# VectorE adds a group's turned rows to X one round later, in the last stage's end of a four-layer kernel

## The chip, the cores and the metric

The kernel runs on one core of one Trainium2 chip. The metric is the device time of one execution in microseconds (us). The time given for a kernel is the median of several runs on the chip; one further execution was profiled, and all rows of the trace come from that one.

## What is computed

Four layers work on x of shape (2, 2048, 128), each wrapped as x + layernorm(layer(layernorm(x))): a time mix, a chain of ternary products, a state space model, and a mixture of experts. Only the last one matters here:

```python
logits = x @ gate_w + gate_b                      # 8 experts
probs = softmax(logits)
top_w, top_idx = top_k(probs, 2)
top_w = top_w / sum(top_w)
h = silu(x @ w1[e]) * (x @ w3[e])
out_e = h @ w2[e]
out = sum over the two experts of top_w * out_e
x = x + layernorm(out)
```

## The kernel before, in words

X stands in SBUF for the whole kernel, features on the 128 partitions and the 4096 positions (2 x 2048) along the free axis. The last stage, phase_moe, sorts the positions by expert, multiplies tiles of 256 gathered rows on TensorE, and scatters the result rows to a table in DRAM (moe_outs), two rows for each position. What follows is the end of the stage, where the change is.

There the 4096 positions go in 8 groups (GROUPS) of 512, each as 4 chunks (TC) of 128 positions. Here a position is a partition and its 128 features lie along the free axis. For each group five engines work one after the other:

- SyncE loads the group's two rows per position from moe_outs (line 1883, 512 KB, a semaphore back0 to back7 for each group; all eight are issued at once). The tile is called room.
- VectorE, add_up (lines 2413 to 2424): the weighted sum of the two rows of each position with its total, four instructions (line 2418), and the negated mean (line 2423, minus). The sums go to `total`, four buffers in the memory of hid, so add_up of group i waits until GpSimd has scaled group i-4.
- ScalarE, spread (line 2128): squares about the mean, four instructions. VectorE, weigh (line 2428), multiplies the sum of squares by the share. ScalarE, inverse_spread (lines 2134 and 2137): Ln and Exp, the inverse root. VectorE, scale_of (line 2433): the factor of the group.
- GpSimd (line 2190), four instructions: (total + minus) * scale, into `scaled`, two buffers in the memory of sq. Group i waits for its factor and, from group 2 on, until TensorE has turned group i-2.
- TensorE (line 2036): turns the four 128x128 blocks by a product with the identity, in f32, into one half of the PSUM tile R1 (pR in the profile), the half i % 2. Group i waits for the scaled rows and, from group 2 on, until VectorE has added group i-2 (semaphore addedC). The profile counts eight matmul records for a group.
- VectorE, add_out (line 2439): X plus the turned rows, 128x512. Then SyncE stores the group's part of X (line 1887, 256 KB).

VectorE's four kinds of work are interleaved by a loop written out by hand, and this sets their order, as each engine works through its instructions in order:

```python
            for i in range(GROUPS + 3):
                if i < GROUPS:
                    add_up(i)
                if 1 <= i <= GROUPS:
                    weigh(i - 1)
                if 2 <= i <= GROUPS + 1:
                    scale_of(i - 2)
                if i >= 3:
                    add_out(i - 3)
```

One pass of this loop is called a round; round i begins with the sums of group i. ScalarE's own loop does spread(i) and then inverse_spread(i-1). GpSimd and TensorE take the groups one after the other.

Of the kernel before, what the change touches and what calls it, by code (L numbers as in the profile page):

```python
# [1741 lines left out]
def phase_moe(nc, G):  # L1742
# [5 lines left out]
    GROUPS = NT * B  # L1748
# [16 lines left out]
    with mem:  # L1765
# [100 lines left out]
        def tile_of(i):  # L1866
            return i % B, ds(i // B)
# [327 lines left out]
        def _(dve):  # L2195
# [202 lines left out]
            for n in range(UNITS):  # L2398
                i, u = divmod(n, 2)
# [12 lines left out]
            def add_up(i):  # L2412
                dve.wait_ge(S[f"back{i}"], 16)
                if i >= 4:
                    dve.wait_ge(S["scaledC"], i - 3)
                for j in range(TC):
                    c = i * TC + j
                    last = nc.vector.scalar_tensor_tensor(out=total[:, i % 4, j, :], in0=back[:, 1, c, :],
                                                          scalar=ratio[:, c:c + 1], in1=back[:, 0, c, :],
                                                          op0=ALU.mult, op1=ALU.add, accum_out=sums[:, c:c + 1])  # L2420
                last.then_inc(S["summed"], 1)
                dve.wait_ge(S["summed"], i + 1)
                nc.vector.tensor_scalar(minus[:, slab(i)], sums[:, slab(i)], -1.0 / P, None, ALU.mult)\
                  .then_inc(S["minus"], 1)

            def weigh(i):
                dve.wait_ge(S["squaredC"], i + 1)
                nc.vector.tensor_tensor(var[:, slab(i)], var[:, slab(i)], squared_share[:, slab(i)], ALU.mult)\
                  .then_inc(S["weighted"], 1)

            def scale_of(i):
                dve.wait_ge(S["rstdC"], i + 1)
                nc.vector.tensor_tensor(scale[:, slab(i)], var[:, slab(i)], share[:, slab(i)], ALU.mult)\
                  .then_inc(S["scale"], 1)

            def add_out(i):
                b, t = tile_of(i)
                dve.wait_ge(S["turnedC"], i + 1)
                nc.vector.tensor_tensor(X[:, b, t], X[:, b, t], R1[:, i % 2, :], ALU.add).then_inc(S["addedC"], 1)

            dve.wait_ge(S["squared_share"], 1)
            for i in range(GROUPS + 3):
                if i < GROUPS:
                    add_up(i)
                if 1 <= i <= GROUPS:
                    weigh(i - 1)
                if 2 <= i <= GROUPS + 1:
                    scale_of(i - 2)
                if i >= 3:
                    add_out(i - 3)  # L2450


# [57 lines left out]
```

## Time and profile before

| | us |
|---|---|
| median of 3 runs | 1417.13 |
| lowest and highest run | 1414.95 and 1420.96 |
| the profiled execution, its own time | 1412.45 |
| its span in the trace | 1410.5 |
| TensorE busy | 1131.2 (80%) |
| VectorE busy | 1012.6 (72%) |
| ScalarE busy | 784.9 (56%) |
| GpSimd busy | 726.6 (52%) |
| mean granted clock of TensorE | 0.90 |

The span runs from the first to the last instruction of the profiled execution; its own time is 1.95 us more. In the rows PE is TensorE, PEld its weight load, DVE VectorE, ACT ScalarE, POOL GpSimd, SP SyncE, and L2418 is line 2418 of the kernel. PEclk is the clock granted to TensorE as a share of its full rate. The last landed scatter stands about 1371.6 us after the start of the span, and the end of the stage runs from there to 1410.5 us. The shares of the whole span say little of it.

### The profile page before, as it was taken

The page shows a single profiled execution, that of the slowest core. Times are in us where ns is not written, and L with a number is a line of the kernel's source. Part 1 is how long each engine was busy: PE and PEld are TensorE (multiplying, and loading weights), DVE is VectorE, ACT ScalarE, POOL GpSimd, SP SyncE. Part 2 cuts the span into 40 slices and gives each one's busy share as a digit, 9 for nine tenths or more (in the row PEclk, how much of TensorE's full clock was granted, in tenths as well). Part 3 has the DMA queues.
Part 4 walks back from the last instruction along what each step waited for, and adds up shares of the span by engine and source line. Part 5 has one row for each costly group of instructions (what it writes and reads, how often), then busy time and mean ns, then how long its engine had stood idle before and what let it go on. Part 6 is the DMA issues. An engine that isn't in the chain of part 4 may idle for free. (4 is left out here: it accounts for less than half of the span.)

```text
span 1410.5 us, 16938 instructions
## 1 busy us (share of the span) xinstructions
PE 1131.2 (80%) x5010; PEld 563.6 (40%) x5010; DVE 1012.6 (72%) x1417; ACT 784.9 (56%) x1269; POOL 726.6 (52%) x611
## 2 busy tenths in 40 slices
PE   6554689999999988888898989896675587877764
PEld 2221234444444333333333333332233475756664
DVE  5996765656645379999999999999927654444444
ACT  5755545646554468686777768674434243333344
POOL 0122351323312038887978888877631466565554
PEclk8886889999999989999999999999986698898885
DMA  6000000000000001000000000000001011111214
GB/s 210 0 1 0 0 1 0 1 1 0 0 0 1 0 31 30 16 16 15 16 16 15 30 0 0 0 0 1 0 8 53 27 39 43 38 41 39 40 52 163
DMA packets 13866, 33.26 MB, mean 24 GB/s; under 512 B 3584, under 2 KB 3776, under 8 KB 13568
## 3 DMA queue, kind: packets, MB, share of 16 engines
q1 hardware_dynamic: 8368, 21.34, 4.5%
q0 software_dynamic: 4992, 10.23, 2.7%
q8 instruction: 39, 0.64, 0.2%
q10 hardware_dynamic: 432, 0.76, 0.2%
q14 instruction: 35, 0.29, 0.1%
HBM read 23.01 MB, written 9.31 MB: 23 GB/s over the span
## 5 line engine op out<-in xcount | busy, mean ns | idle before, releaser
L1632 POOL TENSOR_TENSOR prod<-hs,csb 128x1024 f32<-128x1024 f32 x128 | 301.9, 2359 | 178.0 <-DVE hs L1682 176.7
L1682 DVE TENSOR_TENSOR_SCAN hs<-dA,carry,pD 128x512 f32<-128x512 f32 x256 | 313.8, 1267 | 5.5 <-DVE pD L1697 0.8
L1440 PE MATMUL pY<-prod,const 128*128 128x512 f32 x512 | 245.2, 601 | 11.2 <-DVE h L1667 7.4
L1547 ACT ACTIVATE dA<-dt,negA 128x512 f32<-128x512 f32 x256 | 169.9, 716 | 1.4 <-DVE dt L1734 1.4
L2403 DVE SCALAR_TENSOR_TENSOR hid<-pR,silu 128x512 f32<-128x512 f32 x78 | 53.8, 690 | 131.1 <-ACT silu L2114 83.5
L1440 PEld LDWEIGHTS pY<-prod,const 128*128 128x128 f32 x512 | 96.5, 192 | 122.0 <-issue 107.5
L1558 ACT ACTIVATE csb<-pC 128x512 f32<-128x512 f32 x128 | 76.0, 594 | 108.1 <-PE pC L1453 108.0
L2180 POOL DMA_INDIRECT moe_outs<-y,to x78 | 81.7, 1048 | 85.0 <-ACT y L2106 62.1
L2114 ACT ACTIVATE silu<-pR 128x512 f32<-128x512 f32 x78 | 46.5, 596 | 121.5 <-remote 52.3
L2160 POOL DMA_INDIRECT g<-moe_rows,source x78 | 81.9, 1050 | 48.9 <-DVE source L2352 25.8
L1893 PE MATMUL pR<-x,moe_hi 128*128 128x256 f16 x312 | 93.9, 301 | 15.6 <-DVE x L2387 5.9
L979 ACT ACTIVATE stage<-pR,vec 128x512 f32<-128x512 f32 x64 | 43.9, 687 | 100.1 <-PE pR L679 100.0
L1894 PE MATMUL pR<-x,moe_hi 128*128 128x256 f16 x312 | 93.5, 300 | 3.0 <-issue 3.0
L1895 PE MATMUL pR<-x,moe_lo 128*128 128x256 f16 x312 | 93.1, 298 | 2.7 <-issue 2.4
L1697 DVE TENSOR_TENSOR pD<-dtu,pD 128x1024 f32<-128x1024 f32 x64 | 78.5, 1227 | 6.0 <-PE pD L1450 0.9
L2010 PE MATMUL pY<-moe_hi,hid_lo 128*128 x312 | 64.3, 235 | 11.4 <-issue 11.4
L2009 PE MATMUL pY<-moe_lo,hid_hi 128*128 x312 | 63.9, 234 | 9.0 <-issue 9.0
L1392 PE MATMUL pQ<-xn,convw 128*128 128x512 f32 x112 | 59.1, 653 | 14.7 <-DVE xn L1660 14.7
L1453 PE MATMUL pC<-split,sel 96*128 96x512 bf16 x128 | 50.1, 391 | 24.4 <-ACT csb L1558 24.4
L2008 PE MATMUL pY<-moe_hi,hid_hi 128*128 x312 | 63.9, 234 | 4.9 <-issue 4.1
L1450 PE MATMUL pD<-split,sel 96*128 96x512 bf16 x128 | 50.3, 393 | 21.0 <-DVE hs L1682 20.9
L421 POOL TENSOR_TENSOR o<-o,rs 128x512 f32<-128x512 f32 x8 | 12.3, 1531 | 104.0 <-DVE o L541 104.0
(401 smaller groups left out, 2719.8 us busy)
## 6 DMA issues: line engine op xcount, KB each, us to landing
raw<-moe_w SPq DMA_DIRECT2D x12, 512.0 KB, 3.6
room<-moe_outs SPq DMA_DIRECT2D x8, 512.0 KB, 7.9
hidw<-hid_w SPq DMA_DIRECT2D x1, 2048.0 KB, 10.0
moe_rows<-xt SPq DMA_DIRECT2D x8, 256.0 KB, 2.0
outT<-X SPq DMA_DIRECT2D x8, 256.0 KB, 2.0
X<-xT SPq DMA_DIRECT2D x3, 512.0 KB, 4.2
g<-moe_rows,source POOLq DMA_INDIRECT x78
moe_outs<-y,to POOLq DMA_INDIRECT x78
```

Source lines behind the costliest of these rows:

```text
L1440: last = nc.tensor.matmul(YB[c][:], G.ident, prod[:, slot(b, n), c, :], start=n == 0, stop=n == DST - 1)
L1547: last = nc.scalar.activation(dA[:, slot(b, n), c, :], dt[:, b, c, :], ACT.Exp, scale=negA[:, c, n:n + 1])
L1558: nc.scalar.activation(csb[:, slot(b, n), 0, :], CC[:], ACT.Copy).then_inc(S["c_in"], 1)
L1632: nc.gpsimd.tensor_tensor(prod[:, slot(b, n), :, :], hs[:, slot(b, n), :, :], csb[:, slot(b, n), :, :].to_broadcast([P, CB, N]), ALU.mult)\
L1682: last = nc.vector.tensor_tensor_scan(hs[:, slot(b, n), c, :], dA[:, slot(b, n), c, :], dBu(n, c), carry[:, b, n, c:c + 1], ALU.mult, ALU.add)
L1697: last = nc.vector.tensor_tensor(DD[:, 0:CB, :], dtu[:, b, :, :], bcastB(n).unsqueeze(1).to_broadcast([P, CB, N]), ALU.mult)
L1893: nc.tensor.matmul(out, w_hi, x_hi, start=start, stop=False)
L1894: nc.tensor.matmul(out, w_hi, x_lo, start=False, stop=False)
L1895: return nc.tensor.matmul(out, w_lo, x_hi, start=False, stop=stop)
L2010: last = nc.tensor.matmul(out, hid_lo[:, n % HR, at], w_hi, start=False, stop=u == 1 and h == 1 and r == 1)
L2160: nc.gpsimd.indirect_dma_start(g[:, i % GR, r, :], None, rows, bass.IndirectOffsetOnAxis(ap=source[:, 2 * i + r:2 * i + r + 1], axis=0))\
L2180: nc.gpsimd.indirect_dma_start(outs, bass.IndirectOffsetOnAxis(ap=to[:, 2 * i + r:2 * i + r + 1], axis=0), y[:, i % YR, r, :], None).then_ ...
```

## The change

Only VectorE's loop is changed. The loop has one round more, and the add of a group's turned rows stands at the end of round i+4 in place of round i+3.

```diff
-            for i in range(GROUPS + 3):
+            for i in range(GROUPS + 4):
                 if i < GROUPS:
                     add_up(i)
                 if 1 <= i <= GROUPS:
                     weigh(i - 1)
                 if 2 <= i <= GROUPS + 1:
                     scale_of(i - 2)
-                if i >= 3:
-                    add_out(i - 3)
+                if i >= 4:
+                    add_out(i - 4)
```

The instructions of the other engines and their order are the same. First place: VectorE at round 3, the first that had an add. L2418 are the sums of a group (four instructions), L2423 the mean, L2428 the weighing, L2433 the factors, L2439 the add.

```order
@@ -1060,5 +1060,4 @@
 L2428 TENSOR_TENSOR var<-var,squared_share 128x4
 L2433 TENSOR_TENSOR scale<-var,share 128x4
-L2439 TENSOR_TENSOR X<-X,pR_4 128x512
 L2418 SCALAR_TENSOR_TENSOR hid,sums<-room,ratio 128x128 x4
 L2423 TENSOR_SCALAR minus<-sums 128x4
```

The add of group 0 is gone from between the factors of group 1 and the sums of group 4. In every later round the same five kinds stand in the same places, with the add of the group before.

Second place: VectorE's last rounds, from the factors of group 7 on.

```order
@@ -1085,4 +1084,4 @@
 L2439 TENSOR_TENSOR X<-X,pR_4 128x512
 L2433 TENSOR_TENSOR scale<-var,share 128x4
-L2439 TENSOR_TENSOR X<-X,pR_4 128x512 x2
+L2439 TENSOR_TENSOR X<-X,pR_4 128x512 x3
 L1765 UNCONDITIONAL_BRANCH
```

The factors of group 7 stood behind six adds and two followed; now they stand behind five, and three follow.

## Rows read from the trace of the kernel before

**Rows 1.** The chain that ended last, from 1386 us: start us, us, what

```profile
1386.00 2.15 issue
...
1388.20 2.03 POOL sq L2190 x4
...
1390.28 2.09 PE pR L2036 x8
...
1392.40 2.14 issue
...
1401.51 4.00 PE pR L2036 x16
...
1405.53 0.69 DVE X L2439
```

**Rows 2.** TensorE in order of time, 1380 to 1411 us: [idle before, what ended it]

```profile
1383.87 3.79 PE L2036 MATMUL pR<-const,sq 128*128 128x128 f32 x16 [19.06 <-POOL sq L2190]
1390.28 4.06 PE L2036 MATMUL pR<-const,sq 128*128 128x128 f32 x16 [2.62 <-POOL sq L2190]
1396.68 4.06 PE L2036 MATMUL pR<-const,sq 128*128 128x128 f32 x16 [2.34 <-POOL sq L2190]
1401.51 3.98 PE L2036 MATMUL pR<-const,sq 128*128 128x128 f32 x16 [0.78 <-POOL sq L2190]
```

**Rows 3.** Waits, 1370 to 1411 us: who waited for whom, total, times, longest

```profile
PE pR L2036 <- POOL sq L2190: 24.8, 4, 19.1
POOL sq L2190 <- DVE scale L2433: 18.4, 7, 11.5
...
DVE X L2439 <- PE pR L2036: 10.8, 6, 2.3
```

**Rows 4.** VectorE in order of time, 1386 to 1395 us, same columns as rows 2

```profile
1386.59 0.35 DVE L2418 SCALAR_TENSOR_TENSOR hid<-room,ratio 128x128 f32<-128x128 f32 x1
...
1388.61 0.34 DVE L2418 SCALAR_TENSOR_TENSOR hid<-room,ratio 128x128 f32<-128x128 f32 x1
...
1390.22 0.15 DVE L2433 TENSOR_TENSOR scale<-var,share 128x4 f32<-128x4 f32 x1
1392.39 0.69 DVE L2439 TENSOR_TENSOR X<-X,pR 128x512 f32<-128x512 f32 x1 [2.02 <-PE pR L2036]
1392.99 0.34 DVE L2418 SCALAR_TENSOR_TENSOR hid<-room,ratio 128x128 f32<-128x128 f32 x1
```

**Rows 5.** ScalarE in order of time, 1384 to 1393 us, same columns

```profile
1385.21 0.21 ACT L2137 ACTIVATE var<-var 128x4 f32<-128x4 f32 x1
...
1390.28 0.40 ACT L2128 ACTIVATE convw<-hid,minus 128x128 f32<-128x128 f32 x1 [0.21 <-DVE minus L2423]
...
1392.15 0.20 ACT L2137 ACTIVATE var<-var 128x4 f32<-128x4 f32 x1
```

**Rows 6.** GpSimd in order of time, 1384 to 1393 us, same columns

```profile
1383.80 1.73 POOL L2190 TENSOR_SCALAR sq<-hid,minus,scale 128x128 f32<-128x128 f32 x4
1388.20 2.02 POOL L2190 TENSOR_SCALAR sq<-hid,minus,scale 128x128 f32<-128x128 f32 x4 [2.67 <-DVE scale L2433]
1390.47 1.73 POOL L2190 TENSOR_SCALAR sq<-hid,minus,scale 128x128 f32<-128x128 f32 x4 [0.25 <-DVE scale L2433]
```

**Rows 7.** Line 1883, the eight loads of rows: ns each, first and last start; landing

```profile
L1883 SPq DMA_DIRECT2D room<-moe_outs x8: 552/614/702, 1371.7 to 1376.4; - x8
...
DMA to landing us min/median/max: 4.0/7.9/10.2
```

**Rows 8.** Stretches: busy us of each engine (instructions), PEclk, DMA share, GB/s

```profile
1338.00:1341.70 3.70, 3.70 (x26) 3.02 (x24) 3.09 (x5) 1.91 (x5) 1.72 (x2) 0.51 0.11 22
1341.70:1350.00 8.30, 8.28 (x104) 7.51 (x103) 5.27 (x9) 4.82 (x10) 4.63 (x6) 1.00 0.24 42
1388.00:1411.00 23.00, 12.11 (x48) 10.69 (x48) 9.62 (x45) 8.66 (x42) 10.97 (x24) 0.50 0.23 85
```

**Rows 9.** SyncE's queue about 1406 us: the last store's issue

```profile
1406.25 0.35 SPq L1887 DMA_DIRECT2D outT<-X  x1
```

## The prediction, made before the run

> **What bounds the kernel now.** I read four views in this order. First the time line of the whole program: the change touches nothing before the last stage's end, so 1372 of the 1410.5 us stay as they are, and everything that can be won or lost lies between the first landed sums and the last store. Second, the chain that ended last [rows 1]. The reader should see a pattern there that repeats every 6.40 us and carries two groups: GpSimd scales a group (2.03), TensorE turns it (2.09), and then comes "issue" for 2.15, which is the turn of the other group of the pair; then the next scaling starts. So 1388.20 to 1390.28 to 1392.40, and the same again 6.4 later: 3.2 us per group. Third, TensorE in order of time [rows 2]. It turns the eight groups in four bursts of two, 2.0 us a turn, and before the second, third and fourth burst it stands idle for 2.62, 2.34 and 0.78 us, always until GpSimd has scaled something. That is 5.74 us, and it agrees with the waits of the stretch [rows 3]: 24.8 in total less the first one of 19.1, in which no work had arrived yet.
>
> Why is GpSimd late? It waits for VectorE's factors (18.4 us over 7 times, 11.5 of them the first) and VectorE waits for TensorE (10.8 us, 6 times) [rows 3]. VectorE's order of work shows how [rows 4]: it writes the factors of one group at 1390.22, and then stands for 2.02 us, until the turn that it wants to add is done at 1392.39; only behind that add do the next sums start (1392.99). The factors for the group after next are behind those. It is a ring: turned rows, add, sums, factors, scaling, turning. Every second round of VectorE pays for it. No engine is full: in 1388 to 1411 TensorE is busy 12.11 of 23 us, VectorE 9.62, ScalarE 8.66, GpSimd 10.97 [rows 8].
>
> **The change, part by part.** No instruction is added or removed, and only VectorE's order changes. Its add of group k stood at the end of round k+3 and now stands at the end of round k+4. Call s(k) the sums, f(k) the factors, p(k) GpSimd's scaling, t(k) the turn, a(k) the add.
>
> *The wait in round 3 goes.* Before, a(0) held VectorE until t(0) was done at 1386.0. Now s(4) comes straight behind f(1). It needs p(0) (its buffer of four), which is done when p(1) starts at 1383.80 [rows 6], and its data: loads land 4.0 to 10.2 us after issue [rows 7], and they are issued from 1371.7 to 1376.4, so 0.67 apart; the fifth lands by 1374.4 + 10.2 = 1384.6 at the very worst, and at 1382.3 with the median. So s(4) starts at 1383.85, and 1.6 later VectorE is ready for factors (as from 1388.61 to 1390.22) [rows 4]. ScalarE has the root of group 2 ready at 1385.42 [rows 5], f(2) follows at about 1385.6, and p(2) may start when t(0) has emptied its buffer, 1386.0. Before it started at 1388.20. **That is 2.2 us won in the first step**, and t(2) runs from 1388.06 in place of 1390.28.
>
> *The gaps between the bursts shrink.* A whole round of VectorE without a wait took 2.02 us (1386.59 to 1388.61); made up of the slower round behind it, it is 1.61 to the factors, 0.07 for them and 0.60 for the add (1392.39 to 1392.99), so 2.28 [rows 4]. I take 2.1. A round of ScalarE takes 2.07 (1390.28 to 1392.35) [rows 5], a scaling 2.02 beside sums and 1.73 without [rows 6], a turn 2.0 [rows 2]. All four are near 2.1. Walked on with these: f(3) 1388.05, p(3) 1388.2 to 1390.23, t(3) 1390.28; f(4) 1390.1, p(4) 1390.32 to 1392.35, t(4) 1392.40; p(5) to 1394.17, t(5) 1394.41 right behind t(4); t(6) 1396.42; p(7) needs t(5), 1396.5 to 1398.3; t(7) 1398.43 to 1400.43. The gaps before t(3) and t(4) are 0.2 and 0.1; from t(4) on the turns are back to back and TensorE is the bound. The last add starts at 1400.46 in place of 1405.53 [rows 1]: **5.1 us in all**. The other way to count gives the same: the three gaps of 5.74 less what stays of them, about 0.6.
>
> *Does the later add hurt?* t(k) needs a(k-2) to have emptied its half of the bank, and a(k-2) now stands behind s(k+2) and f(k) in the same round. It ends 0.6 behind f(k), while t(k) must wait for p(k) anyway, 1.73 to 2.02 behind f(k). So the add is covered by the scaling with 1.1 us to spare; if that cover were gone, each turn would wait for what is left of the add, up to 0.6. The stores are issued one by one behind the adds. The turns of a pair end 2.0 apart today, and so come its adds and stores; now all come 2.0 to 2.2 apart; with a DMA share of 0.23 over this stretch [rows 8] that costs nothing. From the last add to the end of the span it was 4.97 us (the add 0.69, a store issued at 1406.25 [rows 9] and its landing), and it stays so.
>
> *What the rows do not show* is GpSimd beside denser VectorE work. The bounds: 1.73 us a scaling without sums next to it, 2.02 with them for two thirds of the time [rows 6]. In the slower one sums ran for 1.3 us beside it (1388.61 to about 1389.9) and cost 0.29, so an us of sums takes 0.22 from GpSimd; with sums beside it all the time a scaling would take 1.73 / 0.78 = 2.2, an estimate from these rows. I take 2.02 up to p(4) and 1.73 behind that, when the sums come to their end. At 2.2 and with VectorE's slow round of 2.28 throughout, groups go at 2.3: p(2) 1386.0 to 1388.0, five more at 2.3 to 1399.5, t(7) to 1401.5, and the gain is 4.0. The Trainium skill, GPSIMD Engine Reference, Key points, has a rule that speaks against this change: GpSimd shares its SBUF interfaces with VectorE and suffers when that has two SBUF inputs, which the sums have. This trace agrees with its 2.02 against 1.73.
>
> The sum against the profiled execution: 1412.45 - 5.1 = 1407.4. That execution was 4.7 faster than the median of the three runs, and the gain does not depend on this, so against the median: 1417.13 - 5.1 = **1412.0 us**, 0.36% less. A measurement of this kernel can tell about 0.5%, or 7.1 us, from no change. So the forecast is a real gain that is too small to see surely.
>
> **The rivals.**
>
> *TensorE's clock rises.* In this stretch the granted clock is 0.50, the lower level of 1.2 GHz [rows 8], and TensorE works in bursts of 4.1 us with idle times of 2.3 to 2.6 between [rows 2]. Now it would turn without a gap worth naming from 1388.06 on. Earlier in the trace, 1338 to 1341.7, it was busy 3.70 of 3.70 at 0.51, and the clock stood at 1.00 from there on [rows 8]. If the same happens, later turns take 1.0 (half of 2.0, an estimate from the two levels). Then GpSimd's 1.73 and VectorE's rounds bound: t(4) 1392.4, p(5) to 1394.17, p(6) 1394.5 to 1396.25, p(7) to 1398.0, t(7) 1398.04 to 1399.06. The gain is 6.4 us, 1410.7. Against it: once turns are short TensorE is busy only half of the time, and the clock may fall again before t(7), which brings it back to 5.1. The Trainium skill, TensorE: Matmul & The Clock Gate, Part 1 (what's actually happening), says that throttled is the default state and that activity releases it. The trace agrees at 1341.7; by that rule alone the result here would be 1410.7.
>
> *GpSimd and VectorE hinder each other* more than today: worked out above, 4.0 won, 1413.1. For it: both engines touch SBUF nearly all the time now. Against it: half of the scalings ran beside sums already and took 2.02.
>
> *The end hangs on something else*, say the stores queue up at the closer spacing, and the last one lands when it did: 1417.1. The low DMA share speaks against it.
>
> *Slower.* The ring closes at another place: a(k-2), now behind s(k+2) and f(k), reaches t(k) too late. It begins to cost when a(k-2) ends more than 1.7 us behind f(k), so when a VectorE round that holds it is 1.1 longer than I think, and the total is a loss once a round exceeds the 3.2 of today. The longest round of the trace, 1388.61 to 1392.99, is 4.38 [rows 4]. If rounds 4 to 7 all took that: 4 x (4.38 - 3.20) = 4.7 lost, 1421.8. But 2.02 of these 4.38 are the very wait for the turn that the change relaxes, so this has little for it.
>
> **How the numbers follow.** Forecast 0.43, clock 0.33, hindrance 0.14, nothing 0.06, slower 0.04. The range: the lower end is the clock's 1410.7 less some 3 for the scatter of medians (the three runs lie 6.0 apart), so 1407.7; the upper end the hindrance's 1413.1 plus 3, and a little more for the case that nothing is won, so 1417.0. Faster by over 0.5% means under 1410.0: the clock's case lies 0.7 away from that and the scatter carries it over in four of ten (0.13), the forecast's lies 2 away (0.08): 0.21 together. Slower by over 0.5%: 0.03, which needs the last case and scatter. The same: 0.76.
>
> **What would show it.** In the changed profile from the start of the second scaling to that of the last add it is 16.7 us, in place of 21.7 (1383.80 to 1405.53). TensorE in order of time shows one burst from about 1388 on in place of three, with no gap over 0.5 us. VectorE's waits for TensorE in the middle rounds shrink from about 2 us to almost nothing, and those of GpSimd for the factors after the first from 6.9 us in total to under 2. If the clock column reads above 0.50 behind 1389, the second case has come. I am wrong if bursts of two with gaps over 1 us remain, if a scaling takes over 2.2 us, or if any turn waits for an add.

## The result and the profile after

The changed kernel takes 1409.87 us (median of 10 runs, 1405.70 to 1412.62) against 1416.22 for the kernel before on the same chip (10 runs, 1412.04 to 1420.96). The ratio is 0.9954, with a 95% interval of 0.9939 to 0.9970. The difference of the medians, 6.35 us, is 0.45%: less than 0.5%, and inside the stated range of 1407.7 to 1417.0. The forecast was 1412.0.

| | before | after |
|---|---|---|
| profiled execution, own time | 1412.45 | 1405.70 |
| span | 1410.5 | 1403.8 |
| first load of line 1883 issued | 1371.71 | 1370.09 |
| from there to the end of the span | 38.8 | 33.7 |
| GpSimd's first scaling starts | 1381.79 | 1379.82 |
| from there to the end of the span | 28.7 | 24.0 |
| mean granted clock | 0.902 | 0.904 |

Of the 6.7 us between the two spans, 1.6 lie ahead of the first load of the tail, where the programs are the same. That is scatter between two executions. From the first load to the end of the span it is **5.1 us** less. But 0.35 of that lies between the first load and GpSimd's first scaling (10.08 us before, 9.73 after), where the order of work is still the same and VectorE waits for the loads: scatter too. From the first scaling on, which is all that the change can touch, it is 4.8 us less in this pair of profiles and 4.6 in a second one (a_copy and b_copy below), so **about 4.7 us**.

The chain that ended last, after (start us, us, what; [rows 1] is its counterpart):

```profile
1379.82 2.03 POOL sq L2190 x4
...
1381.89 2.09 PE pR L2036 x8
...
1384.61 1.25 DVE hid L2418 x8
...
1386.23 0.68 DVE X L2439
1386.90 1.23 DVE hid L2418 x8
...
1388.51 0.68 DVE X L2439
1389.19 1.22 DVE hid L2418 x8
...
1390.77 1.65 ACT convw L2128 x8
...
1392.88 0.17 DVE scale L2433
...
1394.91 1.73 POOL sq L2190 x4
...
1396.68 1.17 PE pR L2036 x8
...
1397.88 0.69 DVE X L2439
```

The 2.15 us of "issue" in [rows 1], which stood for the wait for a turn, are gone. From 1384.61 on VectorE stays in the chain without a stop for three groups: sums 1.25, mean 0.30, add 0.68, next sums. Its adds start at 1386.23 and 1388.51, so a round takes 2.28. Then ScalarE's last squares, two scalings of GpSimd, one turn, one add.

TensorE in order of time, after (as [rows 2]; [idle before, what ended it]):

```profile
1381.89 6.22 PE L2036 MATMUL pR<-const,sq 128*128 128x128 f32 x24 [18.71 <-POOL sq L2190]
1388.49 1.16 PE L2036 MATMUL pR<-const,sq 128*128 128x128 f32 x8 [0.39 <-POOL sq L2190]
1390.77 1.16 PE L2036 MATMUL pR<-const,sq 128*128 128x128 f32 x8 [1.12 <-POOL sq L2190]
...
1396.68 1.16 PE L2036 MATMUL pR<-const,sq 128*128 128x128 f32 x8 [0.57 <-POOL sq L2190]
```

The first burst now holds three turns (24 records), where [rows 2] had two. Behind it the turns stand alone: their length has fallen from 2.0 to 1.16 us, and so there are gaps, up to 1.12 us, which cost nothing. The stretches say why (busy us of the engines, then PEclk, DMA share, GB/s; to be read beside the last of [rows 8]):

```profile
1382.00:1387.50 5.50, 5.33 (x22) 4.74 (x23) 5.24 (x29) 4.88 (x26) 5.10 (x11) 0.50 0.43 161
1387.80:1397.90 10.10, 6.09 (x43) 4.95 (x41) 6.09 (x27) 4.95 (x25) 7.90 (x18) 1.00 0.36 136
```

TensorE was busy for 5.33 of 5.5 us at 0.50, the lower level, and from 1387.8 on it had 1.00, the upper one, up to the last turn.

The waits of the stretch, after (as [rows 3]):

```profile
PE pR L2036 <- POOL sq L2190: 22.7, 6, 18.7
...
POOL sq L2190 <- DVE scale L2433: 12.3, 5, 11.1
DVE X L2439 <- PE pR L2036: 3.0, 4, 1.5
```

VectorE's waits for turns fell from 10.8 to 3.0 us; GpSimd's for factors, less the first, from 6.9 to 1.2. No turn waits for an add. GpSimd in order of time, after (as [rows 6]):

```profile
1384.14 2.02 POOL L2190 TENSOR_SCALAR sq<-hid,minus,scale 128x128 f32<-128x128 f32 x4 [0.15 <-PE pR L2036]
1386.40 2.03 POOL L2190 TENSOR_SCALAR sq<-hid,minus,scale 128x128 f32<-128x128 f32 x4 [0.25 <-DVE scale L2433]
1388.69 2.03 POOL L2190 TENSOR_SCALAR sq<-hid,minus,scale 128x128 f32<-128x128 f32 x4 [0.25 <-DVE scale L2433]
1390.97 1.75 POOL L2190 TENSOR_SCALAR sq<-hid,minus,scale 128x128 f32<-128x128 f32 x4 [0.25 <-DVE scale L2433]
1393.14 3.49 POOL L2190 TENSOR_SCALAR sq<-hid,minus,scale 128x128 f32<-128x128 f32 x8 [0.43 <-DVE scale L2433]
```

From group 2 on the scalings start 2.26, 2.29 and 2.28 apart, in step with VectorE's rounds, and take 2.02 or 2.03 while sums run. The last row is the pair of groups 6 and 7, 3.49 us.

### The profile page after: what moved, and what is told of

Read it like the earlier page. It is cut to its first block and busy times, and to the rows that moved or that the text cites. A ratio compares the mean times of both kernels' runs of the same rounds, so it can differ in the third digit from the quotient of the medians.

```text
span 1403.8 us, 16938 instructions
## 1 busy us (share of the span) xinstructions
PE 1127.7 (80%) x5010; PEld 559.4 (40%) x5010; DVE 1014.2 (72%) x1417; ACT 786.2 (56%) x1269; POOL 727.1 (52%) x611
## 5 line engine op out<-in xcount | busy, mean ns | idle before, releaser
L1029 POOL TENSOR_TENSOR z_lo<-z,z_hi 128x512 f16<-128x512 f32 x8 | 10.6, 1327 | 104.9 <-DVE z_hi L1116 104.9
```

## The experiments

Names that begin with a_ are made from the changed kernel, those with b_ from the one before. Three sets ran on chips of their own, and the kernel before took 1356 to 1357 us in two of them and 1422 in the third, so only ratios and differences within a set are compared. For each run the trace also gives the time from the first load of line 1883 to the end of the span, here called the tail. It leaves the scatter of what runs ahead out (some 1314 to 1387 us). Between the first load and GpSimd's first scaling another 9.6 to 10.4 us pass, which differ from execution to execution whatever the order, so the time from the first scaling to the end is the cleaner measure: the two profiles of the kernel before differ by 0.2 in it, the two of the changed one by less than 0.1. The table was made from the runs and the records of the traces:

```
            runs     ratio to before (95%)        median   tail   first scaling   GpSimd's last scaling   last add's start
                                                  less by         to the end      to the end              to the end
before      -        -                            -        38.8   28.7            7.16                    5.0
b_copy      1        -                            -        39.0   28.6            7.16                    5.1
after       10       0.9954 (0.9939 to 0.9970)    6.4      33.7   24.0            7.15                    5.9
a_copy      12       0.9974 (0.9959 to 0.9988)    3.5      34.0   23.9            7.15                    5.9
a_early     12       0.9960 (0.9945 to 0.9974)    5.3      33.7   24.0            7.16                    5.2
a_warm      12       0.9966 (0.9952 to 0.9979)    4.8      34.1   23.6            7.16                    5.9
a_lag5      12       0.9979 (0.9966 to 0.9991)    3.2      34.3   24.3            7.16                    5.9
a_transp     6       0.9959 (0.9944 to 0.9974)    5.6      33.7   23.5            7.15                    5.9
b_warm      12       0.9992 (0.9978 to 1.0005)    2.2      38.4   28.7            7.16                    5.9
b_transp    12       0.9982 (0.9968 to 0.9995)    3.0      36.2   26.1            7.16                    6.0
a_v7        12       0.9959 (0.9941 to 0.9977)    6.0      32.7   23.1            7.97                    4.3
a_v67       12       0.9967 (0.9949 to 0.9985)    5.0      33.2   22.7            9.87                    4.5
a_v67t      12       0.9958 (0.9940 to 0.9977)    5.9      32.3   22.5            9.66                    4.4
a_pool1      1       -                            -        30.5   20.7            7.15                    5.1
```

Each of the last four columns comes from one profile. The ratios tell the new order from the kernel before, but no version of the new order from another.

The theory at the start of this step: the ring through VectorE's wait for the turn was the bound, and the rise of the clock gave about 1 us on top. The rival: the clock did it.

**a_warm.** 26 products of the identity ahead of the turns, so that the clock is up before the first one.

```diff
+            pe.wait_ge(S["summed"], 1)
+            for _ in range(26):
+                nc.tensor.matmul(R3[:, 0, 0:P], G.ident, G.ident, start=True, stop=True)
             for i in range(GROUPS):
                 pe.wait_ge(S["scaledC"], i + 1)
```

> The changed kernel with 26 extra products of the identity on TensorE (into an unused PSUM bank) from the first group's sums on, so that its clock is up before the first turn. Theory 1 (the ring of turn, add, sums, factors, scaling was the bound, the clock gave about 1 us on top, and it rose soon enough): 1409.4, within 1 us of the changed kernel; all turns about 1.15 us; VectorE's rounds, 2.29 us each, stay the bound. Rival (the clock is what the change brought): at least 2 us faster than the changed kernel, as three more turns become short.

Measured: 0.9966, a tail of 34.1. The first three turns and a part of the fourth ran at the upper clock, then it fell for three of them and came back for the last. From the first scaling to the end it is 0.3 less than in the changed kernel, and no more: short turns at the start, with long ones in the middle, are worth next to nothing. The rival asked for 2 us or more.

**b_warm.** The old order with the same 26 products and, ahead of the turns of groups 2, 4 and 6, another 8, 8 and 3.

```diff
             for i in range(GROUPS):
+                if i in (2, 4, 6):
+                    for _ in range(8 if i < 6 else 3):
+                        nc.tensor.matmul(R3[:, 0, 0:P], G.ident, G.ident, start=True, stop=True)
                 pe.wait_ge(S["scaledC"], i + 1)
```

> The kernel before with the same 26 products ahead, and 8, 8 and 3 of them in the three gaps between its bursts, so that the clock is up for all turns while the order of VectorE is the old one. Theory 1: VectorE still stands for each second turn and then does the next sums, but each turn is 0.9 shorter: 3 to 4 us less than before, 1412.7, and still 2 to 3 us more than the changed kernel; VectorE's waits for TensorE stay, at about 1.1 us each. Rival (the clock is the cause): level with the changed kernel, 1409.9. Second rival (the clock gives nothing): 1416.2.

Measured: 0.9992, an interval that holds 1. From the first scaling to the end it takes 28.7 us, as the kernel before. I had expected 3 to 4 us less. VectorE's waits for the turns are nearly as long as in [rows 3] (10.8):

```profile
DVE X L2445 <- PE pR L2042: 9.4, 7, 3.3
```

But the run is not clean, and cannot decide between the theory and the rival. The first filling was still at work when group 0 had been scaled:

```profile
1323.44 8.42 PE L2033 MATMUL pR<-const 128*128 128x128 f32 x52 [12.32 <-DVE hid L2424]
1331.70 1.95 PE L2042 MATMUL pR<-const,sq 128*128 128x128 f32 x16
```

GpSimd had ended that scaling at 1329.70, so the filling held the first turn up by 2.0 us. That made the longest of VectorE's waits (3.3, against 2.33 before), and the scaling of group 2 starts 7.34 behind the first one, against 6.41 before: 0.9 us lost. The turn of group 4 stood behind a filling as well (scaled at 1342.37, turned from 1343.26), and the clock fell once in between, so that the turn of group 3 took 2.08. What short turns give in the old order is read from b_transp, which has no filling.

**a_lag5.** The add five groups behind the sums.

```diff
-            for i in range(GROUPS + 4):
+            for i in range(GROUPS + 5):
...
-                if i >= 4:
-                    add_out(i - 4)
+                if i >= 5:
+                    add_out(i - 5)
```

> The changed kernel with the add one more round later (five groups behind the sums). Theory 1: in the changed kernel VectorE waits for turns no more than 0.9 us in one place, and that wait lies in round 4; with the turns fast nothing is left to win, so within 0.7 us of the changed kernel (1409.9). If the later add held the turns up, TensorE's waits for VectorE appear and it is slower by 0.5 us or more; if VectorE's wait in round 4 were what is left of the ring, 0.6 us faster.

Measured: 0.9979, and from the first scaling to the end 24.3 us, 0.35 to 0.4 more than the changed kernel's two profiles. TensorE in order of time:

```profile
1326.70 4.12 PE L2036 MATMUL pR<-const,sq 128*128 128x128 f32 x16 [18.94 <-POOL sq L2190]
1331.34 9.55 PE L2036 MATMUL pR<-const,sq 128*128 128x128 f32 x40 [0.53 <-DVE X L2439]
1341.83 1.16 PE L2036 MATMUL pR<-const,sq 128*128 128x128 f32 x8 [0.94 <-POOL sq L2190]
```

The second burst ended an idle time that is put down to VectorE's add: the later add does hold a turn up, once, by 0.53 us. And five turns run on from there in 9.55 us, 1.9 each, so seven of the eight turns are long. Both together cost 0.4 us at most: in the new order the length of the turns hardly counts. The fifth group of distance won nothing, and one turn began to wait for an add. That the kernel is slower by it is not shown, as the ratios overlap.

**a_transp and b_transp.** The turns as transposes, in the changed and in the old order.

```diff
-                    last = nc.tensor.matmul(R1[:, i % 2, j * P:(j + 1) * P], scaled[:, i % 2, j * P:(j + 1) * P], G.ident,
-                                            start=True, stop=True)
+                    last = nc.tensor.transpose(R1[:, i % 2, j * P:(j + 1) * P], scaled[:, i % 2, j * P:(j + 1) * P], G.ident)
```

> The changed kernel with the turns as transposes of TensorE in place of f32 products with the identity. A turn takes well under 1 us, so TensorE leaves the path whatever its clock. Theory 1 with the bound at VectorE's rounds and GpSimd's scalings: 1408.9, 0.5 to 1.5 us less than the changed kernel by the shorter last turn; the clock stays at 0.50, as TensorE is hardly busy. Rival (TensorE is still the bound of the changed kernel): 3 us or more less.

> The kernel before, with its old order, but with the turns as transposes of about 1 us at the low clock. Theory 1: the ring is still there and only its turn is shorter by 1 us; VectorE still waits for each second turn: 3 to 4 us less than before, 1 to 2 us more than the same transposes in the changed order. Rival (order is all): no more than 1 us less than before.

Measured: 0.9959 with 23.5 us from the first scaling to the end, and 0.9982 with 26.1. All turns of a_transp are 1.1 us long, not well under 1 as I had expected, and the clock stays at the lower level over the whole stretch (us, busy us of the engines, PEclk, DMA share, GB/s):

```profile
1330.00:1346.00 16.00, 8.63 (x32) 5.72 (x32) 11.76 (x57) 10.94 (x55) 14.17 (x30) 0.50 0.41 152
```

It ends 0.5 us sooner behind the first scaling than the changed kernel (24.0 and 23.9), without the upper clock. In the old order the short turn wins 2.5 to 2.6 us where I had expected 3 to 4, and the pattern of [rows 2] is still there, TensorE idle for 2.6 and 2.4 us ahead of each second turn:

```profile
1334.19 1.12 PE L2036 MATMUL pR<-const,sq 128*128 128x128 f32 x4 [2.63 <-POOL sq L2189]
1336.17 1.12 PE L2036 MATMUL pR<-const,sq 128*128 128x128 f32 x4 [0.87 <-POOL sq L2189]
1339.64 1.12 PE L2036 MATMUL pR<-const,sq 128*128 128x128 f32 x4 [2.35 <-POOL sq L2189]
```

So with short turns the order is worth 2.6 us (26.1 against 23.5) at one and the same clock, and with the turns as f32 products 4.6 to 4.8. The short turn is worth 2.6 in the old order and 0.5 in the new one. The rival is out: at one clock and one length of turn the order gives 2.6, and with seven long turns (a_lag5) the new order keeps all but 0.4 of its gain. No profile has the new order with f32 turns and the clock at 0.50 throughout; a_lag5 comes nearest.

**a_copy and b_copy.** The two kernels again, unaltered.

> The changed kernel once more, unaltered, beside the others of this set, since the times of a set are read against the kernel before on the same chip. Theory 1: 5 to 6.5 us less than before, ratio about 0.996; TensorE's clock rises again in the middle of the turns. If the rise of the clock is chance, some profile must show it staying at 0.50, with a last add some 1.3 us later, counted from the first scaling.

> The kernel before once more, unaltered, for a profile on this chip. From the first scaling to the start of the last add 23.7 us, bursts of two turns, clock at 0.50 throughout; and from the last add to the end of the span: 5.0 us if the difference seen there belongs to the order of the adds, 5.9 if it is chance.

a_copy is 0.9974 of before, with an interval that overlaps the first one between 0.9959 and 0.9970. From the first scaling to the end it takes 23.9 against 28.6 for b_copy, 4.6 less. So the gain is real and its size is better told by this stretch (4.6 and 4.8) than by the medians, 3.5 and 6.4 less. In b_copy the clock rose too, in the old order, late and for a short time:

```profile
1333.00 4.05 PE L2036 MATMUL pR<-const,sq 128*128 128x128 f32 x16 [2.62 <-POOL sq L2190]
1339.41 3.75 PE L2036 MATMUL pR<-const,sq 128*128 128x128 f32 x16 [2.35 <-POOL sq L2190]
1344.26 1.16 PE L2036 MATMUL pR<-const,sq 128*128 128x128 f32 x8 [1.10 <-POOL sq L2190]
1345.97 1.98 PE L2036 MATMUL pR<-const,sq 128*128 128x128 f32 x8 [0.55 <-POOL sq L2190]
```

The turn of group 6 is short (1.16), that of group 7 takes 1.98 again. From the first scaling to the end that gave 0.2 at most: 28.6 against 28.7. I had expected 0.50 throughout. Whether the clock rises in the old order depends on the execution.

**a_early.** Only the early part of the change: groups 3 and 4 are both added in round 7, and the last rounds are those of before.

```diff
-            for i in range(GROUPS + 4):
+            for i in range(GROUPS + 3):
...
-                if i >= 4:
+                if 4 <= i <= 7:
                     add_out(i - 4)
+                if i >= 7:
+                    add_out(i - 3)
```

> Only the early part of the change: adds of groups 0 to 3 one round later as in the changed kernel, then groups 3 and 4 both in round 7, and the last rounds as before. Theory 1: the gain comes from rounds 3 to 7, where the next sums no longer stand behind a turn; so within 0.7 us of the changed kernel. Rival (the last rounds, in which the factors of group 7 stood behind the add of group 5, hold part of it): 1 to 2 us slower than the changed kernel.

Measured: 0.9960 and 24.0 us from the first scaling to the end, as in the changed kernel. All of the gain comes from rounds 3 to 7. That the factors of group 7 stand behind one add less is worth nothing that can be seen.

**The end of the span.** One number did not fit. From the last add's start to the end it was 5.0 us before and 5.9 after, although the last turn was shorter after. Another one fitted in all ten profiles at that point, whatever the order and the clock: GpSimd's last scaling ended 7.15 or 7.16 us before the end of the span. The line of GpSimd's scalings, before (spans 1410.5) and after (1403.8); the last start is 7.6 ahead of the end in both:

```profile
L2190 POOL TENSOR_SCALAR sq<-hid,minus,scale x32: 445/447/586, 1381.8 to 1402.9; 128x128 f32<-128x128 f32 x32
```

```profile
L2190 POOL TENSOR_SCALAR sq<-hid,minus,scale x32: 447/452/587, 1379.8 to 1396.2; 128x128 f32<-128x128 f32 x32
```

The profile's chain ends with the add on VectorE. But the records that it does not count as work show a DRAIN on GpSimd, its last instruction ahead of the closing barrier. Its record stands from about 9 us before the end until 1.3 before it, and the barrier of all engines closes right behind it:

```
us before the end of the span      before   after
GpSimd's last scaling ends         7.16     7.15
last add starts                    4.99     5.90
SyncE has seen the last store      2.05     2.92
GpSimd's DRAIN ends                1.34     1.33
GpSimd at the closing barrier      1.29     1.29
```

SyncE waited 0.7 us for GpSimd before, and 1.6 after. Three runs test it.

```diff
-            for i in range(GROUPS):
+            for i in range(7):
                 pool.wait_ge(S["scale"], i + 1)
...
+            def scale_rows(i):
+                dve.wait_ge(S["minus"], i + 1)
+                dve.wait_ge(S["scale"], i + 1)
+                dve.wait_ge(S["turnedC"], i - 1)
+                for j in range(TC):
+                    c = i * TC + j
+                    last = nc.vector.tensor_scalar(scaled[:, i % 2, j * P:(j + 1) * P], total[:, i % 4, j, :],
+                                                   minus[:, c:c + 1], scale[:, c:c + 1], ALU.add, ALU.mult)
+                last.then_inc(S["scaledV"], 1)
...
                     scale_of(i - 2)
+                    if i - 2 >= 7:
+                        scale_rows(i - 2)
```

The other two have 6 in place of 7, and the last of them the transposes as well. TensorE waits for scaledV for those groups.

> The changed kernel with the last group's scaling done by VectorE in place of GpSimd. In all ten profiles so far the span ends 7.2 us behind the end of GpSimd's last scaling, while the last add to the end took 5.0 to 6.0. Theory A (the end waits for GpSimd, whose closing barrier comes about 5.9 behind its last scaling, and not for the last store): GpSimd's last scaling is now group 6's, 1.7 us earlier, and the span still ends 7.2 behind it, so 1.7 us less than the changed kernel. Theory B (the end waits for the last store): the scaling of group 7 is shorter on VectorE by about 1 us and the end moves by that, with 5.9 from the last add to the end as before.

> The changed kernel with the scalings of groups 6 and 7 on VectorE. Theory A: GpSimd ends with group 5, 3.9 us earlier than in the changed kernel, and now the last store sets the end: 4.1 to 4.3 from the last add to the end of the span, more than 7.2 from GpSimd's last scaling, and 3 us less than the changed kernel, 8 us less than before. Theory B: 5.9 from the last add to the end stays, 1.5 us less than the changed kernel.

> The same with the turns as transposes. Once the end hangs on the last turn, add and store (Theory A), a shorter last turn counts where the clock is at 0.50: 0 to 1 us less than with the two scalings alone, depending on the clock; 8 to 9 us less than before. Theory B: 1 us less too, so this run only shows what the whole gives.

Measured: in a_v7 GpSimd's last scaling ends 8.0 us ahead of the end, and the last add starts 4.3 ahead, no longer 5.9:

```profile
L2193 POOL TENSOR_SCALAR sq<-hid,minus,scale x28: 446/473/585, 1389.4 to 1404.1; 128x128 f32<-128x128 f32 x28
```

The span is 1412.5, so the last start is 8.4 ahead of it. SyncE has seen the last store 1.33 ahead of the end, and GpSimd's DRAIN had ended at 2.16. So the two have changed places: the end now hangs on the store, as it does in a_v67 (GpSimd's DRAIN ends 4.05 ahead) and a_v67t (3.85). That is Theory A. Its number was too large: I expected 1.7 and 3 us less than the changed kernel, and from the first scaling to the end it is 0.9 and 1.2 less (1.4 with the transposes), since the store takes over after the first of it, and in a_v67 VectorE's own 1.1 us for each group's scaling stands ahead of its adds. The medians, 6.0, 5.0 and 5.9 less than before, do not set any of the three apart from the changed kernel. No version was shown to beat it.

**a_pool1.** GpSimd scales only one of a group's four chunks.

```diff
-                for j in range(TC):
+                for j in range(1):
                     c = i * TC + j
                     last = nc.gpsimd.tensor_scalar(scaled[:, i % 2, j * P:(j + 1) * P], total[:, i % 4, j, :],
```

> The changed kernel with GpSimd scaling only the first of the four chunks of each group; the other three chunks keep what the buffer held, so three quarters of the last layer's contribution to the output are left out. If GpSimd and VectorE hinder each other, VectorE's rounds shrink from 2.29 us to the 2.02 of the undisturbed one. If the rounds are made long by something else (the wait for a turn, ScalarE), they stay near 2.3.

Measured, one run with a profile. VectorE in order of time, the first sums of three rounds:

```profile
1400.86 0.34 DVE L2418 SCALAR_TENSOR_TENSOR hid<-room,ratio 128x128 f32<-128x128 f32 x1
...
1402.88 0.34 DVE L2418 SCALAR_TENSOR_TENSOR hid<-room,ratio 128x128 f32<-128x128 f32 x1
...
1405.05 0.34 DVE L2418 SCALAR_TENSOR_TENSOR hid<-room,ratio 128x128 f32<-128x128 f32 x1
```

They start 2.02 and 2.17 apart in place of 2.22 and 2.28 in the changed kernel (1384.61, 1386.83 and 1389.11). With GpSimd nearly idle the mean takes 0.17 in place of 0.30, and in these rounds no piece of the sums takes over 0.35, where it was 0.45 at times. So GpSimd's work costs VectorE up to 0.26 us a round, about half of it in the mean. With three quarters of GpSimd's work gone the time from the first scaling to the end is 20.7, 3.3 us less. That is no bound for what could be won: the end still hangs on GpSimd's last scaling, 7.2 behind it.

## Why the prediction was right, point by point

**The first step.** "That is 2.2 us won in the first step." With the first load's issue as origin, p(2) was to start 14.3 us behind it (1386.0 less 1371.7); it started 14.05 behind (1384.14 less 1370.09). Behind the first scaling it was to start 4.2 and started 4.3. The sums of group 4 did not wait for their data.

**The walk.** In the same way, p(3), p(4) and p(7) were to start 16.5, 18.6 and 24.8 behind the first load's issue. They started 16.3, 18.6 and 24.8 behind it. GpSimd's last scaling ended 26.5 behind it, against 26.6 in the walk and 31.65 before. That the 5.1 us of the tails equal the forecast's 5.1 is in part luck: the first scaling itself came 0.35 us sooner behind the loads. Counted from it, p(3), p(4) and p(7) started 0.2 to 0.4 later than in the walk, and the gain is 4.7.

**The rounds.** I took 2.1 for a round of VectorE, and it was 2.28, its own bound from the slow side. The walk came out nearly all the same because two errors worked against each other: three rounds were up to 0.2 longer each, and p(7), which in the walk stood until a long t(5) was done, followed p(6) at once. The hindrance case was half right: VectorE's rounds beside GpSimd's work were slow, as a_pool1 shows, but a scaling never took over 2.05. The Trainium skill, GPSIMD Engine Reference, Key points, says that GpSimd shares its SBUF interfaces with VectorE and that the two contend, among others, when a VectorE instruction has two SBUF inputs. The traces agree, and VectorE is slowed too: 2.22 to 2.28 us a round with GpSimd at work, 2.02 to 2.17 with a quarter of that work. But the mean, which has one SBUF input, was slowed as well (0.30 against 0.17). What the prediction ought to have seen is that from p(4) on VectorE's rounds, and not TensorE, were the bound.

**The clock.** Its case came, with a chance of 0.33: the turns fell to 1.16. But its price of 6.4 us was wrong. So the forecast's gain nearly came (4.7 of 5.1) under the conditions of its rival, and that is luck too; what carried it is that in the new order the length of a turn is worth 0.5 us at most. The step of this rival that failed is the last one, "From the last add to the end of the span it was 4.97 us (...), and it stays so." The end did not hang on the last add, neither before nor after. It stood 7.15 us behind the end of GpSimd's last scaling, and the turn, the add and the store behind that had 0.7 us to spare before and 1.6 after. With a long last turn the add starts 2.2 behind that scaling, and this leaves the 4.97; the add does not set it. The 0.9 us of the shorter last turn went into this slack. The shorter turns in the middle did not count as VectorE's rounds were longer. a_transp, with short turns at 0.50, ends 0.5 sooner, and a_lag5, with long turns nearly to the end, 0.4 later.

**What was ruled out.** The slower case: no turn waits for an add in the changed kernel, and it begins to only one step further on (a_lag5, 0.53 us). The longest round before was not 4.38 but 4.99 us, the one from 1381.60 to 1386.59 with the first wait for a turn (2.33), and three scalings of eight, not half of them, took 2.02 or 2.03; neither touches the sum of the forecast. The stores: they landed in 2.0 us as before.

**The signs named.** From the start of the second scaling to the last add I gave 16.7 us in place of 21.7. It is 15.9, by the shorter last turn. "One burst from about 1388 on in place of three, with no gap over 0.5 us" did not come, as the turns were short. The waits came as said (1.2 in place of "under 2").

**The medians.** Their 6.4 against the 4.7 of the profiles stays within the interval, 4.2 to 8.6 us, and the same pair gave 3.5 on another chip. That they equal the 6.4 of the clock's case says nothing for its price: the profiles give 4.8 and 4.6. That the remainder is scatter is the plain reading; it was not tested further.

## What to carry to other kernels

Where an engine that works in order does two jobs in one loop, one that feeds a pipeline and one that collects from its end, place the collecting one far enough behind that it never waits, and no further: here one round more won 4.7 us, and a second one won nothing and made one turn wait. Before a shorter last step is booked as a gain, ask what closes the program; an engine that ended its last work long ago can still hold the closing barrier. And where a change touches 40 of 1400 us, measure that stretch in the trace beside the medians, which scatter by more than it gives.

## What the runs showed of the hardware

GpSimd's DRAIN at the end of the program ends 5.81 to 5.82 us behind the end of its last scaling in all 14 profiles, with 32, 28, 24 or 8 instructions of it, while VectorE's DRAIN ends 0.05 us behind the end of its last add. Why it takes this time is open. Whether it belongs to GpSimd's arithmetic or to the scatters that it had issued some 30 us earlier was not tried.

TensorE's granted clock in the same 20 us of the same program differed from execution to execution: 0.50 throughout and a late rise in two profiles of the kernel before, and in the changed one a rise that held to the end in one profile and fell again in the other. Transposes left it at 0.50.
